# A banded attention mask written by ScalarE instead of multiplied in by TensorE

## The reference, cut to what matters

```python
mask = (it < jb) | (it > jb + w) | (jb == -1)      # w = 32
sim = jnp.einsum('bhwie,bhwje->bhwij', bq, bk2) * QK_SCALE
sim = jnp.where(mask, -jnp.finfo(sim.dtype).max, sim)
attn = jax.nn.softmax(sim, -1)
out = jnp.einsum('bhwij,bhwje->bhwie', attn, bv2)
```

## Time and profile before

| | |
|---|---|
| median of 3 runs | 3683.15 us (3677.87 to 3694.3) |
| the profiled execution | 3697.27 us, its span 3695.5 us |
| busy | PE 94%, PEld 75%, DVE 71%, ACT 59%, POOL 60% |
| chain that ended last | PE 85%, issue 6%, DVE 4%, ACT 3% |
| mean granted clock of PE | 0.981 of full speed |
| mask product L895 | 384 times, 145.6 us busy |
| score products L905 | 24576, 421.5 us busy, and as much again for loads of weights beside them |

### The profile page before, as it was taken

The page is one execution under the profiler, slowest core; times in us unless marked ns, Lnnn a source line. Parts: engine busy times, 40 slices in busy tenths (PEclk is TensorE's granted clock), DMA queues, the critical chain, the costliest instruction groups (busy, mean ns, idle before and its releaser), DMA issues.

```text
span 3695.5 us, 152625 instructions
## 1 busy us (share of the span) xinstructions
PE 3473.6 (94%) x65342; PEld 2754.6 (75%) x65342; DVE 2613.4 (71%) x4403; ACT 2168.3 (59%) x4154; POOL 2206.5 (60%) x2511
## 2 busy tenths in 40 slices
PE   6999999999999999999779999999999999999997
PEld 4777777777777777777667777777777777777775
DVE  4777777777777777777457677767777777777774
ACT  3566665656665666566436656656566666665654
POOL 5656665666566566566246566656656665666552
PEclk8999999999999999999879999999999999999998
DMA  2212221221221221221112122112212212221111
GB/s 78 69 51 53 60 54 47 63 57 45 59 61 47 56 61 50 56 56 50 29 31 66 49 53 65 50 46 64 57 44 61 59 47 56 62 52 46 46 47 34
DMA packets 117863, 197.54 MB, mean 53 GB/s; under 512 B 23756, under 2 KB 36552, under 8 KB 117192
## 3 DMA queue, kind: packets, MB, share of 16 engines
q1 hardware_dynamic: 117192, 187.79, 18.9%
HBM read 33.71 MB, written 1.05 MB: 9 GB/s over the span
## 4 chain that ended last, share of the span: by engine, by line
PE 85%; issue 6%; DVE 4%; ACT 3%; POOL 0%; ACTq 0%; DMA 0%; POOLq 0%; DVEq 0%; SPq 0%
PE s_ps L905 10%; PE tr L964 10%; PE o_ps L947 10%; PE tr L918 6%; PE tr L931 6%; PE qk_ps L847 5%; PE qk_ps L848 5%; PE qk_ps L849 5%; PE tr L874 5%; PE tr L888 4%; PE f_ps L1011 4%; PE s_ps L895 2%; PE tr L847 2%; PE tr L848 2%; PE tr L849 2%
## 5 line engine op out<-in xcount | busy, mean ns | idle before, releaser
L419 POOL TENSOR_TENSOR rotated<-rotated 128x1024 f32<-128x1024 f32 x384 | 908.2, 2365 | 300.2 <-DVE rotated L692 299.1
L686 DVE TENSOR_TENSOR rotated<-qk_ps,rot 128x1024 f32<-128x1024 f32 x384 | 470.3, 1225 | 743.1 <-ACT sq L517 743.1
L440 POOL TENSOR_TENSOR rotated<-rotated,rn 128x1024 f32<-128x1024 f32 x384 | 730.7, 1903 | 30.3 <-POOL rn L432 0.2
L533 ACT ACTIVATE qt<-tr 128x512 f32<-128x512 f32 x384 | 229.5, 598 | 745.1 <-PE tr L874 742.0
L425 POOL TENSOR_TENSOR residue<-guess 128x16 f32<-128x16 f32 x384 | 86.8, 226 | 906.2 <-ACT guess L527 906.2
L692 DVE TENSOR_TENSOR rotated<-qk_ps,rot 128x512 f32<-128x512 f32 x768 | 490.9, 681 | 0.0
L699 DVE TENSOR_REDUCE ss_raw<-sq 128x16 f32<-128x1024 f32 x384 | 464.2, 1209 | 0.0
L905 PEld LDWEIGHTS s_ps<-kt,qt 64*32 64x32 f32 x24576 | 359.5, 107 | 121.6 <-issue 121.4
L964 PE MATMUL tr<-ot,wo 128*128 128x128 f32 x3072 | 434.9, 285 | 4.7 <-issue 3.3
L964 PEld LDWEIGHTS tr<-ot,wo 128*128 128x128 f32 x3072 | 384.1, 193 | 73.0 <-issue 53.3
L947 PE MATMUL o_ps<-vn,pt 64*32 64x65 f32 x12288 | 405.9, 220 | 27.0 <-issue 26.7
(11 more groups left out here) (152 smaller groups left out, 7397.8 us busy)
## 6 DMA issues: line engine op xcount, KB each, us to landing
vs<-vn SPq DMA_DIRECT2D x384, 195.0 KB, 2.6
vs<-vtail SPq DMA_DIRECT2D x384, 65.0 KB, 2.4
vtail<-vn SPq DMA_DIRECT2D x384, 65.0 KB, 2.9
staging<-layer_wqkv_dram SPq DMA_DIRECT2D x72, 256.0 KB, 3.2
wo<-layer_wo_dram SPq DMA_DIRECT2D x12, 512.0 KB, 4.0
xs<-xa SPq DMA_DIRECT2D x48, 128.0 KB, 2.4
fs<-xa SPq DMA_DIRECT2D x48, 128.0 KB, 2.3
xs<-xa SPq DMA_DIRECT2D x48, 127.8 KB, 2.4
```

Of the source, the lines that this page charges most:

```text
L419: nc.gpsimd.tensor_tensor(rot_c[h], rot_c[h], rot_s[h], ALU.add).then_inc(rot_added, 1)
L440: nc.gpsimd.tensor_tensor(folded, folded, rn[:, :].unsqueeze(2).to_broadcast([P, 2 * UH, DH]), ALU.mult).then_inc(qkn_ready, 1)
L686: nc.vector.tensor_tensor(rot_c[h], src, part(0, 0, DH), ALU.mult)
```

## The change

Unit by unit, ACT writes the mask into s_ps with one activation (Copy, bf16 from SBUF to 128x512 f32 in PSUM), and PE's score products add to what they find there. ACT does it between `exps(n - 1)` and `first_guess(n + 1)`, after a wait for dif_ready of unit n - 1. PE's wait for dif_ready and its mask product go; PE waits for a new semaphore, mask_ready, instead. The first unit of each pass (U mod 192 = 0) keeps the product on PE, without a wait for dif_ready.

```diff
@@ -197,6 +197,7 @@
         qt_ready = sem("qt_ready")
         kt_ready = sem("kt_ready")
         s_ready = sem("s_ready")
+        mask_ready = sem("mask_ready")
         max_ready = sem("max_ready")
         dif_ready = sem("dif_ready")
         prob_ready = sem("prob_ready")
@@ -476,7 +477,7 @@
         @block.scalar
         def _(act):
             for released in (sq_ready, qt_ready, kt_ready, prob_ready, pt_ready, vn_ready, ot_ready, fd_ready, fsq_ready,
-                             fn_hi_ready, gate_ready, guess_ready):
+                             fn_hi_ready, gate_ready, guess_ready, mask_ready):
                 act.sem_inc(released, ONE)
             act.wait_ge(consts_in, 48)
             nc.scalar.activation(ident16[:, :], ident[:, :], ACT.Copy).then_inc(consts_ready, 1)
@@ -537,6 +538,12 @@
                 at = WIN + U // 2 % TPS * P
                 nc.scalar.activation(kt[U % 2][:, :, at:at + P], tr1[:, :].rearrange("p (a n) -> p a n", a=PAIRS),
                                      ACT.Copy).then_inc(kt_ready, 1)
+
+            def place_mask(U):
+                act.wait_ge(dif_ready, ONE + U)
+                nc.scalar.activation(s_ps[:, :].rearrange("p (a k) -> p a k", a=PAIRS),
+                                     mask[:, min(U // 2 % TPS, 1), :].unsqueeze(1).to_broadcast([P, PAIRS, 2 * KEYS]), ACT.Copy
+                                     ).then_inc(mask_ready, 1)
 
             def exps(U):
                 act.wait_ge(dif_ready, ONE + U + 1)
@@ -599,6 +606,8 @@
                         queries(n)
                     if live(p, n - 1):
                         exps(n - 1)
+                    if live(p, n) and n % UPP:
+                        place_mask(n)
                     if live(p, n + 1):
                         first_guess(n + 1)
                     if live(p, n):
@@ -891,9 +900,11 @@
 
             def scores(U):
                 h, t = U % 2, U // 2 % TPS
-                pe.wait_ge(dif_ready, ONE + U)
-                nc.tensor.matmul(s_ps[:, :], ident16[:, :], mask[:, min(t, 1), :].unsqueeze(1).to_broadcast([P, PAIRS, 2 * KEYS]),
-                                 start=True, stop=False, skip_group_check=True)
+                if U % UPP == 0:
+                    nc.tensor.matmul(s_ps[:, :], ident16[:, :], mask[:, 0, :].unsqueeze(1).to_broadcast([P, PAIRS, 2 * KEYS]),
+                                     start=True, stop=False, skip_group_check=True)
+                else:
+                    pe.wait_ge(mask_ready, ONE + U - U // UPP)
                 pe.wait_ge(kt_ready, ONE + U + 1)
                 for a in range(PAIRS):
                     for gg in range(2):
```

## The result

The changed kernel took 3718.60 us (median of five, 3715.09 to 3729.12), the kernel before, beside it, 3690.36 (3677.87 to 3694.3). The ratio is 1.0092, with a 95% interval of 1.0067 to 1.0118: slower by 0.9%, some 28 us by the medians and 21 between the two profiled executions (3718.6 and 3697.3). The prediction said 3673.7 and gave 3703 as the upper end.

What follows compares the result with a forecast made beforehand. PE's order of work was taken to set the time, released by ACT's keys' copy in ordinary slots. Terms +14.9, -4.1, -7.7, +8.4, -29.8 and +8.8 summed to -9.5: 3673.7 us on the median, range 3640 to 3703.

Steps and rivals of the forecast that it cites:

- s, the price of the mask product: PE time saved per unit between probability transposes and score products: taken as 0.19 us, at most 0.31.
- Rival (a): Mask product gives back all 0.31 us with a cheap activation, about 3634; chance 0.27 including its other form.
- c, the price of the activation: ACT time added by the mask write between exponentials and logarithm: taken as 0.50 us, bounds 0.45 and 0.62.
- rival (b): ACT bounds every slot at the keys' copy behind the activation, c = 0.62: +33, 3716 us; chance 0.12.
- The later keys: ACT's keys' copy, which releases PE's probability transposes: 0.50 us later in 48 first slots, 0.03 in ordinary ones.
- The DVE loop: Key transposes waiting for DVE's add_output: 102 slots can win only 0.04 us each, -4.1.
- The stops: 110 PE stops at the value products, seemingly tied to the DMA started by ACT's values copy: half of +17.6, +8.8.
- rival (c): All stops at the value products are tied to ACT, so no gain is left: -1, 3682 us; chance 0.09.
- rstd: POOL's rstd comes 0.50 us later in slots n mod 8 = 5; PE stalls 0.42 in 20 of them, +8.4.
- rival (d): PE's clock falls more often as PE has more gaps: 12 more slow stretches, +20, 3694 us; chance 0.07.
- The second form of (a): Only the activation is cheap, c = 0.45: sum -27, less stops -9, 3648 to 3656 us; both forms together 0.27.

Runs made afterwards that it cites:

- without the loop: DVE's add_output moved to right behind differences(n): on the changed kernel, ratio 1.0001 to the kernel before; on the kernel before, 0.999.
- ACT half alone: Kernel before, keeping PE's mask product, plus the same activation at the same place on ACT into an unread SBUF tile: 3737.33 against 3688.93 us, ratio 1.0135.
- PE half alone: Kernel before without any mask product, scores left unmasked, ACT unchanged: 3664.04 us, ratio 0.9937.

## Why the prediction was wrong

- **s, the price of the mask product.** Right: 0.215 measured, 0.19 taken from the pattern with the output transposes. Rival (a), the full 0.31, was wrong, and with it the low end. The Trainium skill's drain (TensorEngine Tiling (Array Packing), Key Properties) agrees with what the trace still shows: 0.56 from four transposes to the small products, where it was 0.46 with the full-size mask product behind them.
- **c, the price of the activation.** Right: 0.52 against 0.50. The condition of rival (b), ACT as the bound from 0.54 on, was not met. Its time of 3716 is close to what was measured, but the mechanism isn't the one that did it.
- **The later keys.** Right: 24 in the first slots of a sequence and 0.03 in each ordinary one, 34 in all before PE's saving. The second stage measured 34, and 36 without the loop. Moving the mask to the head of the slot took it away.
- **The DVE loop.** This step failed. The prediction let 102 slots win 0.04 each in place of 0.16, that is 102 x 0.12 = 12 us of saving eaten by the loop. The distances show 39: 27 at the key transposes and 12 at the gated product. Taking the loop away was worth 34 us in after (give or take 10, by the intervals) and 5 in before (give or take 5), so the change made the loop dearer by some 29. Two things were missed. First, the gated product has its own wait for add_output. Second, the loop begins with ACT's squares, behind the keys, as the prediction says itself; its sum lets ACT's delay into the keys and rstd, and not into the loop. The ACT half alone, with PE's work unchanged, has the gated product 10.7 us later and the key transposes 5.5. The PE half alone has them 5.6 and 19.3 later; for the second, 102 x (0.215 - 0.04) = 18 is what the prediction's own rule gives. What the prediction left out, other slots near the loop, was small: in before 102 key transposes start within 0.1 us of the end of add_output and only 4 more within 0.5; in after 118 start within 0.1.
- **The stops.** This step failed twice. The reason, a transfer started by ACT, fell: the pace is that of the packets of PE's instructions. And the size was halved between "tied to ACT" and "free", +8.8. The distances in the value products grew by 24, which is a stop's slot losing all that PE saves in the stretch: 110 x 0.215 = 24. That lies beyond the 17.6 of rival (c), which had 0.16 for the saving; its size was near and its reason wrong. The queue of kind "instruction" stood on the page of before, and nothing in the prediction draws on it.
- **rstd.** The stall came where it was said, 26 new cases of 0.4 us for 20 forecast. The distances give 12.5 us for the +8.4. What it is worth to the whole is open: 3 us by the ratios, anything from 0 to 10.
- **The clock** (rival (d)) did nothing: 0.982.
- **Slips in the rivals' sums.** The second form of (a) subtracts 9 for stops, which cost time: it should be 3656 to 3665 and not 3648 to 3656. In (b) the stall of 0.54 is that of (a); its own numbers give 0.62 + 0.04 + 0.05 - 0.29 = 0.42, and 2 or 3 us less. Neither changes the forecast.

Side by side, in the prediction's own terms:

| us | prediction | distances between starts |
|---|---|---|
| mask product, 0.19 and 0.215 a unit | -73 | -82 |
| later keys | +34 | +31 |
| DVE loop | +12 | +39 |
| rstd | +8.4 | +12.5 |
| stops | +8.8 | +24 |
| all else | 0 | +1 |
| sum | -9.5 | +26 |

Of the 36 us between the two sums the loop is 27 and the stops 15; the other rows together take 7 back. The right column is one profiled run of each kernel, and it says where PE stood longer, not what would be won by taking one cause away: a wait that is removed can give place to the next, as with rstd. Measured were +28 by the medians and +21 between the profiled runs, whose time outside both passes differs too.

## What to carry to other kernels

Before counting a saving on the busiest engine, find each loop beside it, list every instruction that waits for it, follow it through all engines that the change touches, and ask what paces a stop that ends with "issue". An instruction moved to another engine is free only in that engine's idle time: the same activation cost some 50 us at one place of ACT's order and nothing at another. When a change comes out wrong, a second edit that removes the next wait on both kernels, before and after, tells what the change itself did: here it brought nothing to the one and 0.9% to the other.

## What the runs showed of the hardware

- PE's program arrives in packets of 16,384 bytes, one for 256 of its instructions, here about 126 products. Where 136 products stand in 3.1 to 3.5 us, 85 to 112 of 384 slots stop. A packet has landed 1.2 to 1.6 us before the end of each stop, and the stretch then lasts 4.0 to 4.2 us whether its work takes 3.10, 3.32 or 3.54. Cutting the DMA traffic of the kernel's own transfers from 188 to 62 MB made no difference.
- The mask activation, 128x512 from bf16 in SBUF, took 593 ns into f32 in PSUM and 621 ns at the same place of the ACT half alone, where it writes SBUF (the groups below). From its start to the next it was 0.52 us in both, and for the exponentials, with both ends in SBUF, as well. The Trainium skill (ScalarE: Activation LUTs, Step-by-step) calls PSUM the faster destination; here that is 28 ns of duration, and none of the distance to the next start.

The group of the mask activation in the changed kernel, and that in the ACT half alone (count | busy us, mean ns | idle before):

```profile
L544 ACT ACTIVATE s_ps<-mask 128x512 f32<-128x512 bf16 x382 | 226.4, 593 | 0.0
...
L544 ACT ACTIVATE spare<-mask 128x512 f32<-128x512 bf16 x382 | 237.2, 621 | 0.0
```
